# Experts' first product from rounded parts, in three passes instead of one plain float32 product

## The reference, cut to what matters

```python
scores = jax.nn.softmax(xf @ gate_w.T, axis=-1)        # xf: 1792 tokens x 256
vals, idx = jax.lax.top_k(scores.T, k)                 # k = 224 tokens for each of 8 experts
y = layernorm(xf[flat_idx].reshape(k, n, d)) * ln_w + ln_b
h = jax.nn.gelu(jnp.einsum('knd,nfd->knf', y, fc1s) + b1s, approximate=True)   # 256 -> 1024
out = jnp.einsum('knf,ndf->knd', h, fc2s) + b2s                                # 1024 -> 256
out = out * kept_w[..., None]
xf = xf.at[flat_idx].add(out.reshape(k * n, d))
```

## Time and profile before

| What | Value |
|---|---|
| Runs | 725.01, 727.15, 732.38 us |
| Profiled execution | span 726.4 us, 16788 instructions |
| Experts' stage on PE | from 240.49 to 342.7 us |
| PE busy in the span | 685.5 us (94%) |
| DVE, ACT, POOL busy in the span | 550.9, 361.6, 340.6 us |

### The profile page before, as it was taken

One profiled execution on the slowest core, in us unless ns is written; L12 is line 12 of the kernel. 1 busy time (PEld: TensorE's weight loads), 2 busy tenths in 40 slices (PEclk: granted clock), 3 DMA queues, 4 the chain that ended last, 5 costly groups with the idle time before them and its releaser, 6 DMA issues.

```text
span 726.4 us, 16788 instructions
## 1 busy us (share of the span) xinstructions
PE 685.5 (94%) x6599; PEld 577.1 (79%) x6599; DVE 550.9 (76%) x1192; ACT 361.6 (50%) x699; POOL 340.6 (47%) x232
## 2 busy tenths in 40 slices
PE   8889999999999899999998999999997999999998
PEld 5778788875567899999886776777765887999998
DVE  5688888887867498964568888888888776858464
ACT  2212222226852666564776778778777453232323
POOL 2232433426972488884444787787787000000000
PEclk9999999999999999999999999999999999999999
DMA  9979100003983986671554797778640000000000
GB/s 291 343 227 80 43 26 26 27 25 91 219 195 84 194 266 185 182 235 21 116 136 95 160 184 172 164 171 168 145 104 2 3 1 14 1 26 0 26 14 27
DMA packets 66525, 81.59 MB, mean 112 GB/s; under 512 B 32802, under 2 KB 55938, under 8 KB 65138
## 3 DMA queue, kind: packets, MB, share of 16 engines
q1 hardware_dynamic: 63346, 72.68, 41.6%
q0 software_dynamic: 2816, 3.67, 3.1%
q10 hardware_dynamic: 288, 4.19, 1.4%
HBM read 60.45 MB, written 19.31 MB: 110 GB/s over the span
## 4 chain that ended last, share of the span: by engine, by line
PE 62%; DVE 12%; ACT 10%; DMA 6%; issue 6%; POOL 4%; SPq 0%; DVEq 0%; POOLq 0%; ACTq 0%
PE psum L1274 7%; PE psum L1291 6%; PE psum L2569 6%; PE psum L895 6%; ACT probs L1966 5%; PE psum L1732 5%; DMA kparts_d<-kp 4%; PE psum L360 4%; PE psum L2263 3%; PE psum L2250 3%; PE psum L2222 3%; PE psum L2288 2%; PE psum L931 2%; ACT qpk L1956 2%; PE psum L1740 2%
## 5 line engine op out<-in xcount | busy, mean ns | idle before, releaser
L2057 DVE TENSOR_REDUCE mx<-psum 112x2 f32<-112x750 f32 x128 | 113.2, 925 | 8.1 <-PE psum L2222 7.6
L1966 ACT ACTIVATE probs<-psum 125x448 f32<-125x448 f32 x192 | 91.1, 558 | 16.2 <-PE psum L2250 15.6
L895 PE MATMUL psum<-w_parts,c_parts 128*125 128x512 f32 x282 | 72.8, 409 | 4.2 <-DVE kv L651 4.0
L1873 POOL TENSOR_TENSOR half_sum<-probs 125x896 f32<-125x896 f32 x30 | 62.4, 2081 | 28.5 <-ACT probs L1966 28.5
L895 PEld LDWEIGHTS psum<-w_parts,c_parts 128*125 128x125 f32 x282 | 52.5, 189 | 19.1 <-DVE kv L651 3.7
L2250 PE MATMUL psum<-qpk,kpk 128*128 128x112 bf16 x768 | 60.4, 213 | 4.3 <-ACT probs L1966 4.2
L2222 PE MATMUL psum<-kpk,qpk 96*128 96x375 bf16 x256 | 62.2, 325 | 2.3 <-DVE mx L2057 2.2
L2250 PEld LDWEIGHTS psum<-qpk,kpk 128*128 128x128 bf16 x768 | 45.5, 98 | 23.3 <-issue 7.4
L1879 POOL TENSOR_TENSOR tile_sum<-half_sum,probs 125x896 f32<-125x896 f32 x30 | 62.9, 2098 | 2.3
L1574 ACT ACTIVATE ctx_all<-psum,cols 128x448 f32<-128x448 f32 (+1 forms) x40 | 22.4, 561 | 80.9 <-PE psum L1740 80.9
L1546 POOL TENSOR_TENSOR rs<-ve,mhalf 112x4 f32<-112x4 f32 (+1 forms) x5 | 4.4, 887 | 106.6 <-DVE ve L1589 106.6
(11 more groups left out here) (256 smaller groups left out, 1656.3 us busy)
## 6 DMA issues: line engine op xcount, KB each, us to landing
we<-in_we SPq DMA_DIRECT2D x6, 2048.0 KB, 8.6
kparts_d<-kp SPq DMA_DIRECT2D x16, 562.5 KB, 5.6
kpk<-kparts_d SPq DMA_DIRECT2D x32, 281.2 KB, 4.7
ctx_all<-in_ctxT SPq DMA_DIRECT2D x16, 375.0 KB, 4.0
kpk<-kparts_d SPq DMA_DIRECT2D x32, 187.5 KB, 5.2
we<-in_we ACTq DMA_DIRECT2D x2, 2048.0 KB, 12.9
kpk<-kparts_d SPq DMA_DIRECT2D x32, 93.8 KB, 4.2
qparts_d<-qp SPq DMA_DIRECT2D x16, 168.0 KB, 3.3
```

Of the source, the lines that this page charges most:

```text
L895: ins = pe.matmul(banks[B_KV[t]][0:KT, :], parts_of[:, x, k, t * KT:(t + 1) * KT], w_parts[:, k, w], start=(k == 0 and (x, w) == SPLIT[0]) ...
L1873: pool.tensor_tensor(half_sum[:, m], probs[:, m, 0], probs[:, m, 1], ALU.add)\
L1966: act.activation(probs[:, m, t, g * HU * SQ:(g + 1) * HU * SQ], banks[B_ST[u % 3]][0:KT, 0:HU * SQ], ACT.Exp, scale=SCALE)\
L2057: dve.tensor_reduce(mx[:, n % 2, MAX_AT + 2 * j:MAX_AT + 2 * j + 2], psum[0:SQ, first:first + 2, 0:SK], AX.X, ALU.max)\
```

## The change

The first product is made as the second one was: from high and low parts in three passes, so 16 plain float32 matmuls become 48 with rounded inputs. For this, the next expert's rows get a high part on ACT (the copy that was there, with another type) and a low part on DVE (`rest_of_rows`), and its first weights get a high part on ACT (`round_first_weights`, two halves) and a low part on DVE (`rest_of_first_weights`, two halves). The high parts of rows and first weights have one buffer, so ACT waits for the end of the first product of the expert before. The weights of an expert come in two loads of 1 MB: the first ones once the first product two experts earlier has ended, the second ones as before. `finish` leaves the biased product in PSUM (no `tmp`), so its multiplication reads one input from PSUM. Of the preparations for expert 0, ACT now does the rounding, the first use of GELU and the turned rows between its `keep_value` calls; PE does `turn(0)` before value 6, and the bias row's product after it, into a bank of the outputs. ACT's loop over experts is written out.

```diff
+    w1_in = [wkv0_in.behind(16, 16), loaded.behind(6 * 16, 16)]
+    w2_in = [sem(root, f"w2_in{s}", 16) for s in range(2)]
...
+    we1_low = we_low[:, :, 0:KC * F0].rearrange("p s (k f) -> p s k f", k=KC)
...
+    with ExitStack() as over_z:
+        we1_high = sb(over_z, "we1_high", [128, KC, F0], F32R)
...
-    rT = sb(ctx, "rT", [128, 2, KC, CAP])
+    rT = sb(ctx, "rT", [128, 2, KC, CAP], F32R)
...
-            act.dma_start(we[:, s], d["we"][s]).then_inc(we_in[s].sem, 16)
+            act.dma_start(we[:, s, 0:KC * F0], d["we"][s, :, 0:KC * F0]).then_inc(w1_in[s].sem, 16)
+            act.dma_start(we[:, s, KC * F0:], d["we"][s, :, KC * F0:]).then_inc(w2_in[s].sem, 16)
...
+                sp.wait_ge(fc1_ps.sem, fc1_ps.at(2 * i + s))
+                sp.dma_start(we[:, s, 0:KC * F0], d["we"][2 * i + 2 + s, :, 0:KC * F0]).then_inc(w1_in[s].sem, 16)
                 sp.wait_ge(fc2_ps.sem, fc2_ps.at(2 * i + s))
-                sp.dma_start(we[:, s], d["we"][2 * i + 2 + s]).then_inc(we_in[s].sem, 16)
+                sp.dma_start(we[:, s, KC * F0:], d["we"][2 * i + 2 + s, :, KC * F0:]).then_inc(w2_in[s].sem, 16)
...
-        act.wait_ge(tabs_in.sem, tabs_in.at(2, 0))
-
-        def turned(e, s):
+        def turned(e):
             act.wait_ge(rT_ps.sem, rT_ps.at(e))
-            act.activation(rT[:, s], banks[B_RT][:, 0:KC * CAP].rearrange("p (k c) -> p k c", k=KC),
+            if e:
+                act.wait_ge(fc1_ps.sem, fc1_ps.at(e - 1))
+            act.activation(rT[:, 0], banks[B_RT][:, 0:KC * CAP].rearrange("p (k c) -> p k c", k=KC),
                            ACT.Copy).then_inc(rT_done.sem, 1)
 
+        def round_first_weights(e, i, s):
+
+            act.wait_ge(w1_in[s].sem, w1_in[s].at(i))
+            if e:
+                act.wait_ge(fc1_ps.sem, fc1_ps.at(e - 1))
+            for h in range(2):
+                half = slice(h * F0 // 2, (h + 1) * F0 // 2)
+                act.activation(we1_high[:, :, half], we1[:, s, :, half], ACT.Copy).then_inc(we1_split.sem, 1)
...
-                turned(e + 1, 1 - s)
+                turned(e + 1)
+                round_first_weights(e + 1, i + s, 1 - s)
                 round_weights(e + 1, i + s, 1 - s)
 
+        for b in range(3):
+            keep_value(act, b, 0)
+        act.wait_ge(z_out.sem, z_out.at(PAIRS - 1))
+        act.wait_ge(total_out.sem, total_out.at(PAIRS - 1))
+        round_first_weights(0, 0, 0)
+        keep_value(act, 3, 0)
         round_weights(0, 0, 0)
-        turned(0, 0)
-        for s in range(2):
-            step(0, s, False, first=(s == 0))
-        with act.Fori(1, E0 // 2 - 1) as i:
+        keep_value(act, 4, 0)
+        act.activation(first_gelu[:], mhalf[0:1, 0:1], ACT.Gelu_apprx_tanh)
+        keep_value(act, 5, 0)
+        turned(0)
+        keep_value(act, 6, 0)
+        act.wait_ge(tabs_in.sem, tabs_in.at(2, 0))
+        for i in range(E0 // 2):
             for s in range(2):
-                step(i, s, False)
-        step(E0 // 2 - 1, 0, False)
-        step(E0 // 2 - 1, 1, True)
+                step(i, s, (i, s) == (E0 // 2 - 1, 1), first=((i, s) == (0, 0)))
...
+        def rest_of_rows(e):
+            dve.wait_ge(rT_done.sem, rT_done.at(e, 1))
+            dve.tensor_tensor(rT[:, 1], banks[B_RT][:, 0:KC * CAP].rearrange("p (k c) -> p k c", k=KC),
+                              rT[:, 0].bitcast(F32), ALU.subtract).then_inc(rT_done.sem, 1)
+
+        def rest_of_first_weights(e):
+            s = e % 2
+            for h in range(2):
+                half = slice(h * F0 // 2, (h + 1) * F0 // 2)
+                dve.wait_ge(we1_split.sem, we1_split.at(e, 2))
+                dve.tensor_tensor(we1_low[:, s, :, half], we1[:, s, :, half], we1_high[:, :, half].bitcast(F32),
+                                  ALU.subtract).then_inc(we1_split.sem, 1)
...
-            dve.tensor_tensor(tmp[:, s], banks[B_OUT[s]][0:SQ, :].rearrange("p (h w) -> p h w", h=2),
-                              spread(b2[:, e], 1, 2), ALU.add).then_inc(tmp_done.sem, 1)
-            dve.wait_ge(tmp_done.sem, tmp_done.at(e))
-            dve.tensor_tensor(outs[:, s], tmp[:, s], spread(weight_now[:, s], 2, D), ALU.mult)\
+            product = banks[B_OUT[s]][0:SQ, :].rearrange("p (h w) -> p h w", h=2)
+            dve.tensor_tensor(product, product, spread(b2[:, e], 1, 2), ALU.add).then_inc(biased_done.sem, 1)
+            dve.wait_ge(biased_done.sem, biased_done.at(e))
+            dve.tensor_tensor(outs[:, s], product, spread(weight_now[:, s], 2, D), ALU.mult)\
                 .then_inc(outs_done.sem, 1)
 
         for s in range(2):
             one_hots(0, s, first=True)
             find(0, s)
-        dve.tensor_tensor(rows1[0:SQ, 0:D], rows1[0:SQ, 0:D], banks[B_IDX][0:SQ, 128:128 + D], ALU.add)
+        rest_of_first_weights(0)
         one_hots(1, 0)
+        rest_of_rows(0)
+        dve.wait_ge(fc1_ps.sem, fc1_ps.at(0, 1))
+        dve.tensor_tensor(rows1[0:SQ, 0:D], rows1[0:SQ, 0:D], banks[B_OUT[1]][0:SQ, 0:D], ALU.add)
         for s in range(2):
             keep(0, s, True)
             rest_of_hidden(0, s)
+            rest_of_rows(1 + s)
             find(1, s)
+            rest_of_first_weights(1 + s)
             one_hots(1 + s, 1 - s)
...
-            pe.wait_ge(we_in[s].sem, we_in[s].at(i))
             pe.wait_ge(rT_done.sem, rT_done.at(e))
             for f in range(FC):
                 g = f // 2
+                if f % (FC // 2) == 0:
+                    pe.wait_ge(we1_split.sem, we1_split.at(e, f // (FC // 2) + 3))
                 if f % 2 == 0 and not first:
                     pe.wait_ge(h_low_done.sem, h_low_done.at(e - 1))
                 for k in range(KC):
-                    ins = pe.matmul(banks[B_F[g]][:, (f % 2) * CAP:(f % 2 + 1) * CAP],
-                                    we1[:, s, k, f * 128:(f + 1) * 128], rT[:, s, k],
-                                    start=(k == 0), stop=(k == KC - 1))
+                    for w, x in SPLIT:
+                        chunk = slice(f * 128, (f + 1) * 128)
+                        ins = pe.matmul(banks[B_F[g]][:, (f % 2) * CAP:(f % 2 + 1) * CAP],
+                                        we1_low[:, s, k, chunk] if w else we1_high[:, k, chunk], rT[:, x, k],
+                                        start=(k == 0 and (w, x) == SPLIT[0]),
+                                        stop=(k == KC - 1 and (w, x) == SPLIT[-1]))
...
-                pe.wait_ge(tmp_done.sem, tmp_done.at(e - 1, 0))
+                pe.wait_ge(outs_done.sem, outs_done.at(e - 1, 0))
...
-        for m in range(KC):
-            pe.matmul(banks[B_IDX][0:SQ, 128:128 + D], bv1[:, m:m + 1].broadcast_to([128, SQ]), wo1[:, m],
-                            start=(m == 0), stop=(m == KC - 1))
         pe.wait_ge(parts_done.sem, 4)
         find(0, 0)
         value(pe, 3, range(NKT), 0)
         value(pe, 4, (0,), 0)
         find(0, 1)
         value(pe, 4, (1, 2), 0)
-        for b in range(5, V_EARLY):
-            value(pe, b, range(NKT), 0)
+        value(pe, 5, range(NKT), 0)
         turn(0, 0)
+        value(pe, 6, range(NKT), 0)
+        for m in range(KC):
+            pe.matmul(banks[B_OUT[1]][0:SQ, 0:D], bv1[:, m:m + 1].broadcast_to([128, SQ]), wo1[:, m],
+                            start=(m == 0), stop=(m == KC - 1))
...
```

More of the change, by code:

```diff
@@ L81, in __init__, with behind @@
     def __init__(self, ctx, nc, name, per=1):
-        self.sem, self.per = ctx.enter_context(nc.semaphore(name)), per
+        self.sem, self.per, self.base = ctx.enter_context(nc.semaphore(name)), per, 0
     def at(self, n, k=None):
-        return n * self.per + (self.per if k is None else k)
+        return self.base + n * self.per + (self.per if k is None else k)
+    def behind(self, done, per):
+        later = Sem.__new__(Sem)
+        later.sem, later.per, later.base = self.sem, per, done
+        return later
 class Chain:
@@ L153, in two_layer_kernel @@
     later_in = sem(root, "later_in", 16)
-    we_in = [sem(root, f"we_in{s}", 16) for s in range(2)]
+    wkv0_in = sem(root, "wkv0_in", 16)
+    w_split = sem(root, "w_split", 1 + 2 * KC)
+    w1_in = [wkv0_in.behind(16, 16), loaded.behind(6 * 16, 16)]
+    w2_in = [sem(root, f"w2_in{s}", 16) for s in range(2)]
     waited_v = sb(root, "waited_v", [1, 1])
@@ L233, in two_layer_kernel @@
         rs3 = sb(ctx, "rs3", [SQ, 3, 2])
-        wkv0_in = sem(ctx, "wkv0_in", 16)
         rows_in = sem(ctx, "rows_in", 16)
-        w_split = sem(ctx, "w_split", 1 + 2 * KC)
         high_done = sem(ctx, "high_done")
@@ L278, in two_layer_kernel @@
     ctx = ExitStack()
+    sb(ctx, "under_we1_high", [128, KC * F0 - 4 * D])
     iota = sb(ctx, "iota", [SQ, CAP], BF16)
@@ L294, in two_layer_kernel @@
     h_high = sb(ctx, "h_high", [128, FC, CAP], F32R)
-    tmp = sb(ctx, "tmp", [SQ, 2, 2, D])
     outs = sb(ctx, "outs", [SQ, 2, 2, D])
@@ L529, in _ @@
                 act.activation(token5[:, :, 3], rest[:], ACT.Copy).then_inc(parts_done.sem, 1)
-        for b in range(V_EARLY):
```

(31 more changed lines are left out.)

## The result

| | before | changed |
|---|---|---|
| median | 728.13 us (4 runs, 725.01 to 732.38) | 743.92 us (4 runs, 740.31 to 747.74) |
| ratio | 1 | 1.0179, 95% interval 1.0139 to 1.0218 |
| profiled span | 726.4 us | 745.9 us |
| experts' stage on PE | 240.49 to 342.7 | 237.59 to 356.5 |

The change makes the kernel 1.8% slower. The forecast was 732.7 us with a range of 721 to 741, so the sign was right, the time lies outside the range, and what happened is the second rival. The profiled execution of the changed kernel is the slowest of its four (747.74 us), so numbers from the profile lie about 4 us above the median. Two runs in what follows, one of e1 (843 us) and one of the kernel before (1706 us), fell into a much slower state and are left out of the ratios.

The account below looks back on a forecast made before the run. PE bound the experts' stage at 13.0 us per expert; DVE, held by POOL, would take 14.6. Stage +6.9 and -1.4 ahead of it give +5.5: span 731.9, 732.7 us on the median's scale, range 721 to 741.

Parts of the forecast that it names:

- the sign: Whole kernel: the change makes it slower, by 5.5 us in total.
- the second rival: Experts' stage: POOL gets in between two one-hots, DVE is held the full 4.53 us, 16.1 us per expert; 740 us, chance 0.23.
- PE's part: First product in the experts' stage: 48 matmuls take 5.36 us against 6.05; PE's expert becomes 12.3 us.
- ACT's part: Experts' stage: high parts of first weights add 2.0 us, ACT becomes 9.8 of 12.3 us; costed at nothing.
- the earlier load: Experts' stage: loading first weights earlier costs nothing, as it lands before it is asked for.
- DVE's own sum: Experts' stage: DVE's operations without holding sum to 11.6 us per expert, which alone fits into 12.3.
- one-hots and POOL's subtraction exclude each other: Experts' stage: one-hots block with POOL's L1132 as L1207 did; cost bounded between nothing and 4.53 us per expert.
- So I take POOL to wait to the end of the one-hots: Experts' stage: 1.6 us of L1132 lie beside bias, outs and keep, DVE waits 2.9 us; 14.6 us per expert used.
- The clock: Ahead of the experts' stage: PE's half-clock stretch while values 4 were made may shift 1.7 us either way; costed at nothing.
- The gain ahead of the stage: Before expert 0's first product: preparations move under PE's values, ending at about 239.1 against 240.49, -1.4 us.
- the case that I had named: Ahead of the stage: a loss of 0.4 us if L1132 takes its turn before DVE's low rows of expert 0.
- the chance of "slower": Whole kernel: a time above 734.4 us, from rival 2 and a quarter of the forecast; chance given as 0.36.

Follow-up runs that it names:

- e1: The changed kernel with the tokens' positions (pos1) in PSUM, so a one-hot reads one input from SBUF and one from PSUM; 726.14 us, ratio 0.9923.
- e9: The kernel of e1 with SP's 18 key loads spread, 3 behind the second weights of each of the 6 reloads; 719.41 us, ratio 0.9848.
- e2: The kernel before with only a pause of two memsets on DVE, about 2.4 us, ahead of the one-hots of experts 3 to 7; 743.23 us, ratio 1.0191.
- e3: The changed kernel with POOL's subtraction of the second weights cut to one of 8 chunks; 725.30 us, ratio 0.9940.
- e8: The kernel before with only the biased product kept in PSUM and multiplied from there; 732.32 us, ratio 1.0033.
- e7: The changed kernel with 22 idle products on PE between the first product and the wait for the one-hots; 744.59 us, ratio 1.0203.

## Why the prediction was wrong

- **PE's part: right.** Forecast 5.36 us for 48 matmuls from the earlier trace rows; the blocks last 5.51 us with the tail of the last matmul, against 6.22 read the same way before, so 0.7 us less. Where nothing holds it, PE's expert is 12.28 us (e9), forecast 12.3.
- **ACT's part and the earlier load: right** in that neither set the pace; ACT is at 9.5 us of 15.7, forecast 9.8.
- **DVE's own sum: right.** Forecast 11.6 us. The cycle is 292.88 - 277.16 = 15.72 us, less the 4.5 us of hold 11.2.
- **That one-hots and POOL's subtraction exclude each other: right**, though no row of the kernel before showed a one-hot held. e1, e2 and e3 show it from three sides. The Trainium skill, "SBUF — State Buffer", § Who interferes with whom, gives the rule for two SBUF inputs without an exception for a type; bf16 one-hots agree (5.59 us against 1.08).
- **"So I take POOL to wait to the end of the one-hots": wrong. This is the step that failed.** I read it from one operation that had come out long and so let 1.6 us of the hold lie beside bias, outs and keep: 14.6 us per expert. POOL had its turn at the next border between instructions in every one of the five experts with one-hots, nothing lay beside the hold, and the cycle is 15.72. That is 5 x 1.12 = 5.6 us of the miss. It was also not so that a POOL operation met a run of DVE's only once in the trace: the gathers beside the one-hots did so for expert after expert (1.68 us against 1.04, above), and they got in at a border. The same section of the Trainium skill says that issue order decides who blocks; here the trace agrees with it as a queue, and I had weighed one unclear row above it. What held xb for 1 us in the earlier trace rows stays open; no run was made on it.
- **The clock and the late gather were not in the sum.** Experts 1 to 5 took 18.1 + 14.0 + 17.3 + 14.2 + 18.4 = 82.0 us against 5 x 14.6 = 73.0. Of the 9.0, 5.6 are the hold. Of the other 3.4, 2.7 are the second product of expert 5 at a lower clock (8.62 us against 5.9), behind which no more one-hots stand to cover it, and 0.35 the late gather, behind which DVE's one-hots began 16.07 us apart instead of 15.72. Expert 0 took 14.0 instead of 12.4, its first product also at a lower clock, behind a pause of 2.1 us. Experts 6 and 7 took 23.0, forecast 23.7: POOL has no gather left in expert 6, so its list didn't hold it at 12.3. Together 1.6 + 9.0 - 0.7 = 9.9 us over the forecast of the stage (119.0 us against 102.2 + 6.9).
- **The gain ahead of the stage: wrong by the case that I had named.** From the first one-hot to the first product it took 22.9 us before (217.59 to 240.49) and 23.1 us after (214.52 to 237.59): +0.2, not -1.4. POOL's subtraction for expert 0 ran at 229.46, the one-hots beside it took 8.47 us, and DVE's low rows stood behind them. In e9, where this hold is gone, it takes 20.9 us (211.6 to 232.54): -2.0, a little more than the -1.4 of the forecast.
- **Outside the stage** the two profiles differ by -3.1 us before the first one-hot and by +5.7 behind the experts (383.7 to 389.4 us). The granted clock goes the same ways: over the first 200 us it was 0.98 before and 1.00 in the changed kernel, and behind the experts three stretches of 60 us had 0.97 where all had 1.00 before, which would make about 3 x 60 x 0.03 = 5.4 us, an estimate. The change hardly touches those parts, no experiment was made on them, and the first difference varies between kernels by more than its size (first one-hots at 210.8 to 217.6 us). I don't attribute them. On the scale of the profiles the whole miss is 19.5 - 5.5 = 14.0 us: 9.9 in the stage, 1.6 ahead of it, 2.6 outside; by the medians it is 11.2.
- **The chances.** The rival that came true had 0.23 and 740 us; my range ended in its middle. Two outcomes that differ only in who is served first deserved nearly equal chances on one unclear row. And by its own terms the chance of "slower" was 0.23 and a quarter of 0.42, 0.34 and not 0.36.

## What to carry to other kernels

Before a step is put in front of another on DVE, list which of its operations read two inputs from SBUF and when POOL wants to read SBUF: the two lists add up (11.2 + 4.5 us here) although neither engine is full, and the hold counts in full unless only operations with an input in PSUM stand beside it. A tiny copy from SBUF to SBUF was held too (4.08 us for two elements in e8), so moving one operation out of the way can leave the hold to the next. Look also for short POOL instructions beside DVE's in the trace you have: the gathers of the kernel before showed who is served next. The cheapest cure is placement: a small operand that is read often, moved to PSUM, took 18 us out of this kernel. And when a stage gets faster, bulk loads for later stages that share its DMA engines have to be spread (725.75 to 719.41 us), or one late gather takes back what was gained.

## What the runs showed of the hardware

- A one-hot of 112x896 takes the same with one operand in PSUM (1.080 us) as with both in SBUF (1.084), and isn't held by a POOL operation that runs over it.
- In a run of DVE operations with two SBUF inputs, POOL's waiting operation is served at the next border. The subtraction asked 0.1 to 0.2 us ahead of one each time and then held DVE for all its 4.5 us; DVE's hold follows the length of POOL's operation (4.5 us for 2048 columns, 0.64 for 256).
- A gather's instruction on POOL that began inside a DVE operation with two SBUF inputs took what was left of this operation and 0.9 us more (1.63 and 1.68 us in the kernel before, 1.81 in the changed one, 2.00 in e9), 1.04 beside a one-hot with an input in PSUM (in the repeat of e1) and 1.03 to 1.06 with DVE idle. It didn't lengthen the DVE operations behind it.
- A copy of 2 elements per partition from SBUF to SBUF was held too, until POOL's subtraction ended: 4.08 us in e8, up to 3.50 in e1 and e9, 3.17 in the changed kernel (expert 7), against 0.16. In e9 it took 0.33 us at 286.44, where POOL's operation ended at 286.73.
- In the changed kernel PE's pauses of 2.2 to 2.5 us ahead of find came before stretches at half the granted clock (0.50), 3.4 us long in one expert and about 7 us in two (second products of 7.4 to 8.6 instead of 5.9 us); behind pauses of 0.6 to 0.7 us the second products took 5.9 us. With idle products in the pause (e7) every second product of the held experts took 5.9 us.
